# Moving the second layer norm of five token tiles from the attention half into the feed-forward half

## The reference, cut to what matters

```
h   = layernorm(x) * (1 + ca) + sa
x1  = x + ga * attention(h)            # 16 heads, 4 memory banks, one output projection
xn2 = layernorm(x1)                    # the "second norm": the part that is moved
h2  = xn2 * (1 + cb) + sb
a   = silu(h2 @ w_gate) * (h2 @ w_up)  # width 2048
a   = the 2 largest |a| of each group of 4, the others zero
out = x1 + gb * (a @ w_down)
```

## Time and profile before

| | us |
|---|---|
| median of 3 runs | 1370.35 (1369.13 to 1370.67) |
| the profiled execution, its own time | 1369.18 |
| its span, first to last instruction | 1367.4 |
| TensorE busy | 1344.9 (98%) |
| VectorE busy | 849.0 (62%) |
| ScalarE busy | 638.1 (47%) |
| GpSimd busy | 564.4 (41%) |

### The profile page before, as it was taken

One profiled execution on the slowest core, in us unless ns is written; L12 is line 12 of the kernel. 1 busy time (PEld: TensorE's weight loads), 2 busy tenths in 40 slices (PEclk: granted clock), 3 DMA queues, 4 the chain that ended last, 5 costly groups with the idle time before them and its releaser, 6 DMA issues.

```text
span 1367.4 us, 18629 instructions
## 1 busy us (share of the span) xinstructions
PE 1344.9 (98%) x6726; PEld 1099.4 (80%) x6726; DVE 849.0 (62%) x1212; ACT 638.1 (47%) x933; POOL 564.4 (41%) x428
## 2 busy tenths in 40 slices
PE   7999999999999999999999999999999999999998
PEld 6777777777788888888888888888888888888887
DVE  6878888876756363645555565765555546363646
ACT  6677777787543343334333344533333343343311
POOL 2877777771733241414141456553231323231412
PEclk9999999999999999999999999999999999999999
DMA  6422222236302020202030323322020202020102
GB/s 256 155 89 97 86 75 84 92 93 193 108 16 85 15 84 15 84 15 84 15 96 34 100 74 104 108 70 85 15 84 15 84 15 84 15 84 15 69 0 100
DMA packets 91422, 102.43 MB, mean 75 GB/s; under 512 B 68960, under 2 KB 69504, under 8 KB 84864
## 3 DMA queue, kind: packets, MB, share of 16 engines
q1 hardware_dynamic: 91392, 102.05, 22.9%
HBM read 51.69 MB, written 33.57 MB: 62 GB/s over the span
## 4 chain that ended last, share of the span: by engine, by line
PE 86%; DVE 8%; ACT 2%; issue 2%; POOL 1%; DMA 1%; SPq 0%; DVEq 0%; ACTq 0%; POOLq 0%
PE bank L1247 27%; PE bank L1249 27%; PE bank L1248 27%; DVE banks_r L1061 3%; PE bank L1322 2%; DVE inv_norm L1049 1%; PE bank L1334 1%; POOL h_lo L457 1%; PE bank L1275 1%; DMA wmod_sb<-in_wmod_dram 1%; PE bank L1298 1%; DVE ln_raw L889 0%; DVE h_abs L1193 0%; DVE xn L985 0%; ACT h_abs L795 0%
## 5 line engine op out<-in xcount | busy, mean ns | idle before, releaser
L1152 DVE TENSOR_TENSOR h_act<-bank,silu_g 128x512 f32<-128x512 f32 x128 | 88.3, 690 | 411.7 <-PE bank L1249 385.6
L506 POOL TENSOR_TENSOR hs_lo<-h_abs,hs_hi 128x512 fp32r<-128x512 f32 x124 | 170.1, 1401 | 381.4 <-ACT hs_hi L774 381.4
L774 ACT ACTIVATE hs_hi<-h_abs 128x512 fp32r<-128x512 f32 x124 | 72.7, 628 | 323.5 <-DVE h_abs L1193 200.6
L457 POOL TENSOR_TENSOR h_lo<-h_raw,h_hi 128x512 fp32r<-128x512 f32 x62 | 122.2, 1999 | 233.2 <-ACT h_hi L757 233.2
L1247 PE MATMUL bank<-h_hi,gate_w_hi 128*128 128x512 f32 x512 | 199.8, 390 | 1.7 <-POOL h_lo L457 1.4
L1247 PE MATMUL bank<-h_hi,up_w_hi 128*128 128x512 f32 x512 | 199.6, 390 | 0.3 <-DVE h_act L1152 0.2
L1248 PE MATMUL bank<-h_lo,up_w_hi 128*128 128x512 f32 x512 | 199.2, 389 | 0.0
L1248 PE MATMUL bank<-h_lo,gate_w_hi 128*128 128x512 f32 x512 | 199.2, 389 | 0.0
L1249 PE MATMUL bank<-h_hi,gate_w_lo 128*128 128x512 f32 x512 | 199.2, 389 | 0.0
L1249 PE MATMUL bank<-h_hi,up_w_lo 128*128 128x512 f32 x512 | 199.2, 389 | 0.0
L1247 PE MATMUL bank<-down_w_hi,hs_hi 128*128 128x512 f32 x496 | 192.9, 389 | 0.0
(11 more groups left out here) (149 smaller groups left out, 2478.6 us busy)
## 6 DMA issues: line engine op xcount, KB each, us to landing
x_ring<-in_x_dram SPq DMA_DIRECT2D x8, 1024.0 KB, 4.9
x_scratch<-x_ring SPq DMA_DIRECT2D x8, 1024.0 KB, 3.9
xn_bits_scratch<-set_up_stage SPq DMA_DIRECT2D x8, 1024.0 KB, 4.5
over_x<-x_scratch SPq DMA_DIRECT2D x8, 1024.0 KB, 4.9
acc_scratch<-over_x SPq DMA_DIRECT2D x8, 1024.0 KB, 3.9
over_x<-acc_scratch SPq DMA_DIRECT2D x8, 1024.0 KB, 4.9
out_dram<-over_x SPq DMA_DIRECT2D x7, 1024.0 KB, 3.9
w_raw<-in_w_gate_dram SPq DMA_DIRECT2D x4, 1024.0 KB, 5.9
```

The lines of the kernel that those rows point to most:

```text
L457: nc.gpsimd.tensor_tensor(h2_lo[:, k], h2_raw[:, k], h2_hi[:, k].bitcast(F32), ALU.subtract).then_inc(h2_lo_done, 1)
L506: nc.gpsimd.tensor_tensor(hs_lo[:, j], h_abs[:, j], hs_hi[:, j].bitcast(F32), ALU.subtract).then_inc(hs_lo_done, 1)
L774: nc.scalar.activation(hs_hi[:, j], h_abs[:, j], ACT.Copy).then_inc(hs_hi_done, 1)
L1152: nc.vector.tensor_tensor(h_act[:, cc, j], bank[2 * (j % 2) + 1][:], silu_g[:, j % 2], ALU.mult).then_inc(h_done, 1)
```

## The change

`EARLY = 3`: the second norm of tiles 0, 1 and 2 stays where it was. For tiles 3 to 7 the statistics, aggregation, scalars, normalization, bit split and bit store are taken out of the first half and out of the entry to the second. In the second half's passes t2 = 1 to 5 each pass does the norm of tile t2 + 2, one subtile at a time: ScalarE issues a load of 128 x 512 from `x1_scratch` into one buffer (`late_x1`), VectorE takes its statistics, ScalarE the square root, VectorE the two scalars, ScalarE normalizes in place, splits the bits into one buffer (`late_bits`) and issues their store; then it issues the load of the next subtile. SP's load of the next bits waits for the four stores of that tile. SP's waits for `xn2_done` before x loads and weight loads go where the norm went.

```diff
 # ScalarE
+            def late_load(tile, s):
+                act.wait_ge(bits_done, 4 * tile + s)
+                nc.scalar.dma_start(late_x1[:], x1_t[tile, :, s]).then_inc(late_in, 16)
+            def late_root(tile, s):
+                act.wait_ge(ag2_done, 4 * tile + s + 1)
+                nc.scalar.activation(late_sd[:], late_mv[:, 1:2], ACT.Sqrt, bias=eps_col[:]).then_inc(sd_done[1], 1)
+            def late_split(tile, s):
+                index = 4 * tile + s - 3 * EARLY
+                act.wait_ge(shift_done[1], index + 1)
+                nc.scalar.activation(late_x1[:], late_x1[:], ACT.Identity, bias=late_shift[:],
+                                     scale=late_rstd[:]).then_inc(xn2_done, 1)
+                act.wait_ge(xn2_done, 4 * tile + s + 1)
+                act.wait_ge(bits_out, 16 * index)
+                words = late_x1[:].bitcast(U16).rearrange("p (k d h) -> p k h d", k=K, h=2)
+                nc.scalar.activation(late_bits.rearrange("p (k h d) -> p k h d", k=K, h=2), words,
+                                     ACT.Copy).then_inc(bits_done, 1)
+                act.wait_ge(bits_done, 4 * tile + s + 1)
+                nc.scalar.dma_start(bits_dram[tile][s * P:(s + 1) * P], late_bits).then_inc(bits_out, 16)
+                if s < S - 1:
+                    late_load(tile, s + 1)
+            def tile_b(t2, tile=None, last=False, late=False):
+                def between(cc):
...
+                    def join_and_root():
+                        join_h2(t2 + 1, tile, 2 * cc + 1)
+                        late_root(t2 + 2, 2 * cc)
+                    return {0: join(2 * cc), 1: join_and_root, 2: lambda: late_split(t2 + 2, 2 * cc),
+                            3: lambda: late_root(t2 + 2, 2 * cc + 1)}
+                if late:
+                    late_load(t2 + 2, 0)
                 hs_high(2 * t2 - 1)
+                item(2 * t2, 0, between(0))
+                if late:
+                    late_split(t2 + 2, 1)
                 hs_high(2 * t2)
+                item(2 * t2 + 1, 1, between(1))
+                if late:
+                    late_split(t2 + 2, 3)
                 if not last:
                     act.wait_ge(up_done, 8 * t2 + 8)
                     h2_high(t2 + 1)
...
 # VectorE
+            def late_norm(tile, s):
+                dve.wait_ge(late_in, 16 * (4 * (tile - EARLY) + s + 1))
+                nc.vector.bn_stats(late_raw[:], late_x1[:]).then_inc(bn2_done, 1)
+                dve.wait_ge(bn2_done, 4 * tile + s + 1)
+                nc.vector.memset(late_pad[:], 0.0)
+                nc.vector.bn_aggr(late_mv[:], late_raw[:]).then_inc(ag2_done, 1)
+            def late_scalars(tile, s):
+                index = 4 * tile + s - 3 * EARLY
+                dve.wait_ge(sd_done[1], index + 1)
+                nc.vector.reciprocal(late_rstd[:], late_sd[:]).then_inc(rstd_done[1], 1)
...
                     for j in range(J):
                         hidden_act(n, cc, j)
+                        if late and j == 0:
+                            late_norm(t2 + 2, 2 * cc)
+                        if late and j == 2:
+                            late_scalars(t2 + 2, 2 * cc)
+                        if late and j == 3:
+                            late_norm(t2 + 2, 2 * cc + 1)
...
                         sparsify(n, cc)
+                        if late:
+                            late_scalars(t2 + 2, 2 * cc + 1)
...
 # SP
+                if late:
+                    sp.wait_ge(bits_out, 16 * (EARLY + 4 * (tile - EARLY + 1)))
```

More of the change, by code:

```diff
@@ L300, in store_bits, with load_bits @@
                 sp.dma_start(bits_dram[t].rearrange("(s p) c -> p s c", p=P), xn2_bits).then_inc(bits_out, 16)
-            def load_bits(t2, half, tile=None):
+            def load_bits(t2, half, tile=None, late=False):
                 tile = t2 if tile is None else tile
+                if late:
+                    sp.wait_ge(bits_out, 16 * (EARLY + 4 * (tile - EARLY + 1)))
                 sp.dma_start(bitsT.rearrange("p k h n -> p (k h) n"), bits_dram[tile][:, half * D:(half + 1) * D],
@@ L364, in _ @@
                 sp.wait_ge(bits_joined, 4 * t + 8)
-                load_bits(t + 2, 0)
+                load_bits(t + 2, 0, late=True)
             t = NT - 2
@@ L675, in copy_row, with tile @@
                 nc.scalar.activation(mod_rows[:, i], bank[5 + 2 * i][:, 0:P], ACT.Copy).then_inc(rows_done, 1)
-            def tile(t, first=False, last=False):
+            def tile(t, first=False, last=False, norm2=False):
                 for s in range(S):
@@ L701, in tile @@
                             h1_split(t + 1, before_last=transposed, part=None if first else 1)
-                        if not first and not last:
+                        if norm2:
                             ln_sqrt(t - 1, 1)
@@ L705, in tile @@
                     if s == 3:
-                        if not first and not last:
+                        if norm2:
                             split_bits(t - 1, (0, 1))
                         transposed()
-                        if last:
-                            normalize(t - 1, 1, xn2, xn2_done)
-                            split_bits(t - 1, (0, 1))
                     if last and s == 0:
@@ L721, in tile @@
                         h2_high(0, (s + 1,))
-                    if last and s == 2:
-                        ln_sqrt(t - 1, 1)
                     if first and s == 3:
@@ L727, in h2_rest @@
                 def h2_rest():
-                    if not first:
+                    if norm2:
                         split_bits(t - 1, (2, 3))
-                if last:
-                    h2_rest()
-                else:
+                if not last:
                     sigma_all(t + 1, between=h2_rest, before_high=lambda: combT_high(4 * t + 3, 1))
@@ L762, in _ @@
             act.wait_ge(mods_ready, 2)
-            with act.Fori(1, NT - 1) as t:
+            with act.Fori(1, EARLY + 1) as t:
+                tile(t, norm2=True)
+            with act.Fori(EARLY + 1, NT - 1) as t:
                 tile(t)
@@ L809, in join @@
+            def tile_b(t2, tile=None, last=False, late=False):
                 def join(k):
                     return lambda: join_h2(t2 + 1, tile, k)
+                def between(cc):
+                    if last:
+                        return {}
+                    if not late:
+                        return {0: join(2 * cc), 1: join(2 * cc + 1)}
+                    def join_and_root():
[5 more added lines that the diff above has]
+                    late_load(t2 + 2, 0)
@@ L846, in _ @@
             h2_high(1)
-            with act.Fori(1, NT - 1) as t2:
-                tile_b(t2, t2 + 1)
+            act.wait_ge(x1_out, 16 * NT)
+            with act.Fori(EARLY - 2, NT - 2) as t2:
+                tile_b(t2, t2 + 1, late=True)
+            tile_b(NT - 2, NT - 1)
             t2 = NT - 1
@@ L1134, in tile @@
                                                 ALU.subtract).then_inc(h2_lo_done, 1)
-                late_stats(t, 0, u)
-                attn_rest(t, 1, u + 1, between=lambda: combT_low(u + 2, 0))
+                if t < EARLY:
+                    late_stats(t, 0, u)
+                attn_rest(t, 1, u + 1, between=lambda: combT_low(u + 2, 0), stats=t < EARLY)
                 if first:
@@ L1204, in add_ffn, with tile_b @@
                     nc.vector.tensor_tensor(y[:, s], bank[4 + s][:], y[:, s], ALU.add).then_inc(y_done, 1)
-            def tile_b(t2, last=False):
+            def late_norm(tile, s):
[8 more added lines that the diff above has]
+                nc.vector.reciprocal(late_rstd[:], late_sd[:]).then_inc(rstd_done[1], 1)
+                dve.wait_ge(rstd_done[1], index + 1)
+                nc.vector.scalar_tensor_tensor(out=late_shift[:], in0=late_mv[:, 0:1], scalar=-1.0, in1=late_rstd[:],
+                                               op0=ALU.mult, op1=ALU.mult).then_inc(shift_done[1], 1)
+            def tile_b(t2, last=False, late=False):
                 for cc in range(SLOTS):
@@ L1236, in _ @@
             sparsify(1, 1)
-            with dve.Fori(1, NT2 - 1) as t2:
+            with dve.Fori(EARLY - 2, NT - 2) as t2:
+                tile_b(t2, late=True)
+            with dve.Fori(NT - 2, NT2 - 1) as t2:
                 tile_b(t2)
```

45 lines of the change are left out of this document (22 added, 23 removed).

## The result

| | before | changed |
|---|---|---|
| median of 4 runs, us | 1370.51 | 1451.33 (1450.56 to 1451.53) |
| ratio | 1 | 1.0594 (1.058 to 1.0607) |
| profiled execution, its span | 1369.18, 1367.4 | 1450.56, 1448.8 |
| mean granted clock of TensorE | 0.999 | 0.975 |

A forecast was written before the change was run, and what follows sets the result against it. TensorE, busy 98% of the span, was taken to bound the kernel, a solid wall in the second half. 1369.2 - 3.0 (first half) + 78.5 (five passes) + 5 (clock) = 1449.7, so 1450 us; range 1415 to 1482.

The forecast's parts named there:

- The new waits: Second half: second and fourth splits wait for post-sparsify scalars, second and fourth statistics for loads; TensorE idles 12.0 and 1.8.
- The landing: Late passes: a 256 KB load from the stored sum lands in 3.4 us, the fourth subtile's in 4.4; bounds 2.5 and 5.8.
- Issue: Late passes: issuing a DMA on ScalarE takes 0.37 us, bounds 0 and 0.43.
- Clock: TensorE's granted clock drops after the stall in each late pass: 5 us for five, bounds 0 and 8.
- The first half: Norm work removed from the first half and the second half's entry wins only visible waits: 3.0 us, bounds 0 and 5.
- The table switch: ScalarE's late norms: each table load costs 1.28 us, before the square root and before the next Silu, without a drain.
- the rule: The Trainium skill's 2.66 us a table switch, 1.38 of it drain; as first rival it gave 1485, chance 5%.
- the passes: Five late passes in the second half take 81.0 us each in place of 65.3, costing 78.5 in all.
- One sign: Sign of being right: VectorE waits 2 to 4 us for a DMA before each second and fourth statistics.

The follow-up runs named there:

- the removal alone: Changed kernel with the second norm of tiles 3 to 7 left out and no late norm in the second half: 1364.68 us (0.9963).
- the last version: Changed kernel with h2_high ahead of the fourth split, two load buffers, and one square root and scalar pair for two subtiles: 1364.56 us (0.9962).

## Why the prediction was right, step by step

The chain of one pass, from the issue of the fourth split's store (446.2 in the changed kernel's trace), forecast against measured:

| step | forecast | measured |
|---|---|---|
| h2_low complete | 5.8 | 5.8 |
| last up block of the first item ends | 25.5 | 26.8 |
| last absolute ends | 28.5 | 29.9 |
| sparsify starts, ends | 32.0, 41.8 | 33.0, 42.7 |
| first Silu of the second item ends | 49.1 | 50.3 |
| last absolute ends | 63.8 (63.2 + 0.6) | 65.0 |
| sparsify starts, ends | 68.3, 78.1 | 70.3, 80.0 |
| fourth store issued | 80.9 | 82.9 |

- **The new waits.** Both are where they were put, in size too: 12.0 us forecast ahead of the first gate block, 12.5 to 12.9 measured; 1.8 and 1.7 ahead of the third. Moving the scalars alone took back 54 us; moving scalars, h2_high and one square root took back 81 of the 86.7, with the amount of work unchanged: shown, not argued.
- **The landing.** 3.4 forecast for the second subtile, 3.4 from issue (474.96) to statistics (478.34). For the fourth 4.4, measured 5.6 (510.03 to 515.64), and 5.5 to 5.8 in all five passes. SP issues the reload of y 1.8 us before it; that this is the reason was not tested by itself. It is 1.2 us a pass, the largest error in the chain.
- **Issue.** 0.35 to 0.41 on ScalarE's queue against 0.37; but the next instruction starts 1.1 to 1.2 behind the engine's last for two issues, where I had 0.8.
- **Clock.** Right in sign, too large by more than half: 5 us in the sum, 2.2 measured. The pass of this table is the one that loses most, 1.0 us, and its first item ends 1.3 late. From 0.83 as a mean of one window in the set-up the prediction took about 1 us a stall; but most of what a lower clock would cost is hidden, as the first gate block goes at GpSimd's pace anyway, which the prediction named and then counted too little for.
- **The first half.** 3.0 forecast, 5.3 measured by the removal alone: mis-sized. The starts of tiles show where: one tile of the first half takes 35.02 (250.14 to 285.16) where it took 35.65 (251.00 to 286.65), so 0.63 is won and not the 0.21 of the wait table; the first pass of the second half takes 65.71 in the run with the removal alone where it took 67.31. The table counts idle time between matmuls whose ends are modelled; a short stall can show only in the distance of starts. The upper bound of 5 took that in, nearly; the value taken did not.
- **The table switch.** The rows were right against the rule: the trace shows the load of 1.28 and the next activation 0.02 behind it, and taking away all switches was worth 14 us, where 2.66 a switch would have given 25 or more. The 2.66 us of the Trainium skill (ScalarE: Activation LUTs, What ACT_TABLE_LOAD costs) are not seen in any of these runs. The Trainium skill's advice to batch activations by set (ScalarE: Activation LUTs, Table sets: the hidden batching unit) is what the last version follows: 20 loads in its late passes instead of 45, and none between hs_high and the first Silu of a pass. What that is worth by itself was not measured.
- **What cancelled.** Without the clock, the passes cost 84 us and not 78.5 (landing, issues). The clock gave 2.8 of this back and the first half 2.3. So the mechanism and the two waits were right, but that the total came within 1.3 us of the measured one is luck; each error by itself lay inside the range.
- **One sign was off.** VectorE was to wait 2 to 4 us for a DMA before the second and fourth statistics; it waits 4.4 and 7.1. The prediction's own chain gives about 4.7 and 6.5 there: the sign was written down wrongly, the chain was not.
- **What I missed**, though it did not touch the number: a second wait, that of the square root for the load, stood ahead of h2_high too, hidden behind the longer one. It made two of my expectations of the experiments (1403 and 1367) wrong by 34 and 30 us.

## What to carry to other kernels

Where one engine is a wall, ask of each instruction put into another engine's queue not what it costs but what stands behind it and when that is wanted: here the wait ahead of 0.3 us of square root cost 26 us. With all waits behind what the wall waits for, 20.1 us of added ScalarE work a pass (24.1 before, 44.2 busy) cost 0.8 to 1.3 us, and 13.0 us (37.1 busy) in the last version cost nothing. When the longest wait in front of an instruction is taken away, the next one in the same queue takes its place: list them all before pricing the repair. Read stalls of a pipelined engine from the distance of starts, not only from the table of waits.

## What the runs showed of the hardware that was not expected

- The late passes hold 45 table loads and not 40: at the head of each pass one stands in front of a Copy (line 780) that runs without one at 492.36, and its own stands again in front of the Silu. The one ahead of a square root that waits for VectorE runs early (511.19, the square root 516.59); the one ahead of the Silu behind a matmul's wait began only when that wait had ended (2.00 us idle at 454.02), so it adds its 1.28 us to the Silu's latency.
- A 256 KB load issued on ScalarE's queue lands in 3.5 us as a median (3.1 to 5.8 over the 20), a 256 KB store in 2.1.
- Two DMA issues keep ScalarE's next activation 1.1 to 1.2 us away, though each is shown as 0.35 to 0.41.
- At the five restarts behind stalls of 12.5 to 12.9 us the granted clock is at 0.50 and returns to 1.00 while TensorE is still fed at GpSimd's pace, so this costs only 0.1 to 1.0 us each.
- VectorE and GpSimd slow each other: pair_lo takes 1.22 us alone and 2.31 beside h2_low, and four blocks of h2_low take 5.0 alone and up to 8.25 beside the sparsify.
